# Layer 0 of a graph network on one core: found tiles from two float32r parts of x, four in every batch

## The chip, the core and the metric

The kernel runs on one core of a Trainium2 chip. A core has TensorE (PE, matrix multiply; PEld is its weight load), VectorE (DVE), ScalarE (ACT), GpSimd (POOL, which here issues the indirect DMAs) and SyncE (SP, which issues the plain DMAs). The engines run their own instruction streams and meet at semaphores. The metric is device time in microseconds (us), from one execution to the next; lower is better.

## The reference

12,500 nodes with 32 features and 200,000 edges, sorted by target node. Layer 0 averages the features of the source nodes into each target node; layer 1 is an equivariant message passing whose per-edge weights come from a small network of the edge weight; each layer is followed by a residual and a layer norm.

```
def _L0_gnn_ref(hn, src, dst):
    msgs = hn[src]
    sums = jax.ops.segment_sum(msgs, dst, num_segments=N_NODES)
    deg = jax.ops.segment_sum(jnp.ones((dst.shape[0],), dtype=hn.dtype), dst, num_segments=N_NODES)
    return jnp.where(deg[:, None] > 0, sums / jnp.maximum(deg[:, None], 1.0), 0.0)
...
edge_index = jnp.stack([src, dst])
x = _layernorm(x + _L0_gnn_ref(x, src, dst), axis=-1)
x = _layernorm(x + _L1_gnn_ref(x, edge_weight, edge_attr_3, edge_index, w1, b1, w2, b2), axis=-1)
```

What matters here is `hn[src]`, the row of x for each edge, in float32.

## The kernel before

Each of the 128 partitions owns 1564 consecutive edges, cut into 98 batches of T = 16 edge columns. Batches go in pairs: k = 0 is the even one, k = 1 the odd one. Layer 0 takes 47 pairs in a mixed way, and then two pairs whose rows are all gathered. In a mixed batch some of the 16 tiles (a tile is one column of 128 edges) are gathered from memory by POOL, one indirect DMA of 128 rows each (line 547), and the others are found by TensorE: 3 in an even batch, 4 in an odd one (`FOUND = (3, 4)`), so that POOL gathers 25 a pair.

A found tile is a product with a one-hot matrix. x lies on chip as 128 partitions by 98 nodes. PE first spreads the edges' row codes over the partitions (`spread_codes`, lines 783 and 785, into the bank `rows`). DVE compares them with the block's row numbers and so writes the one-hot `hot_s` (line 1163, into the room `hid`). PE multiplies it with the three bfloat16 parts of x (hi, mid, lo, in the rooms `rest_f`, `inv_len` and `w_sb`), 7 blocks times 3 parts, which makes 21 matmuls of 448 columns into one PSUM bank (`find`, line 800). DVE then multiplies the bank with a second one-hot, `hot_l` (`select`, line 1173), and after the batch's last tile a reduction over it (line 1177) puts the rows into the batch's terms. A carry (line 1241) and a scan along the edges (line 1246) close the batch. PE also counts edges per node with 16 small matmuls a batch (`count`, line 771) out of `hot_p` and `hot_j`, which DVE writes (lines 984 and 986).

Three PSUM banks take found tiles, `found[g % 3]` for the g-th tile of a batch. In an odd batch the fourth tile goes into the first one's bank, so PE waits until that one has been selected (`pe.wait_ge(selected, FOUND_PAIR * i + g + 1)`); in an even batch it waits once, at the first tile, for every earlier selection.

The order of the work is written out by hand. On DVE a batch b is: hot_p, hot_j, hot_l, then hot_s of batch b + 1, then the selections of batch b one after another, the reduction, the carry, the scan. After an odd batch comes a piece of the frames of layer 1 (`frame_piece`, lines 1191 to 1231, one of seven in turn). On PE it is: spread_codes of b + 1, find of b, count of b. POOL issues its gathers in order; those of a batch wait for steps of a find five or so batches earlier (`found_steps`, `AHEAD = 5`), and for their slot, one of seven.

Ahead of the loop x is split: ACT writes hi, DVE writes left = x - hi, mid and lo (`split_x`, lines 1150 to 1155). `w_sb` becomes free for lo only when ACT has copied the last turned block of it (`w_copied`).

Of the kernel before, what the change touches and what calls it, by code (L numbers as in the profile page):

```python
# [25 lines left out]
NPP = 98  # L26
# [8 lines left out]
DEEP = 7  # L35
FOUND = (3, 4)
FETCHED = tuple(T - n for n in FOUND)
FOUND_PAIR = sum(FOUND)
# [49 lines left out]
def build_program(nc, x, src, dst, edge_attr, edge_weight, w1, b1, w2, b2, out):  # L88
    with ExitStack() as ctx:
        def sb(name, shape, dt=F32):  # L90
            return ctx.enter_context(nc.sbuf_tensor(name, shape, dt))
# [7 lines left out]
        def dram(name, shape):  # L99
# [12 lines left out]

        src_all = sb("src_all", [P, COLS + 2 * DEEP * T], I32)
        dst_i = sb("dst_i", [P, COLS], I32)
        dst_f = sb("dst_f", [P, COLS])
        rest_f = sb("rest_f", [P, COLS])
        same = sb("same", [P, COLS])
        unit = sb("unit", [P, COLS, 3])
        inv_len = sb("inv_len", [P, COLS])
        w_sb = sb("w_sb", [P, COLS])  # L120
        x_room = sb("x_room", [P, T * D * MUL])
# [39 lines left out]
        runs_t = [sb(f"runs_t{k}", [P, T, D]) for k in range(2)]  # L161
        frame = [sb(f"frame{k}", [P, T, 3, 3]) for k in range(2)]
        frame_b = [sb(f"frame_b{k}", [P, T, 3, 3]) for k in range(2)]
        hot_p = [sb(f"hot_p{k}", [P, T, P], BF16) for k in range(2)]
        hot_j = [sb(f"hot_j{k}", [P, T, NPP], BF16) for k in range(2)]
        f_along = [sb(f"f_along{k}", [P, T, 2, 2, MUL]) for k in range(2)]
        f_across = [sb(f"f_across{k}", [P, T, 2, 2, MUL]) for k in range(2)]
        hid = [sb(f"hid{k}", [P, T * P]) for k in range(2)]
        halves = [room.rearrange("p (v t o) -> p v t o", t=T, o=D) for room in
# [33 lines left out]
        sq = prod[0][:, :, :, :, :].rearrange("p a b c d -> p (a b c d)")  # L203
        part = sb("part", [P, 3, T, 3, MUL])
        back = sb("back", [P, 3, T, 3, MUL])
        span_room = x1_sb[:, :, :].rearrange("p j f -> p (j f)")
        frame_s = span_room[:, 0:SPAN * 9].rearrange("p (t c a) -> p t c a", c=3, a=3)
        small = span_room[:, SPAN * 9:SPAN * 14].rearrange("p (c t) -> p c t", t=SPAN)
        parts = [room[:, :].bitcast(BF16) for room in (rest_f, inv_len, w_sb)]
        hot_s = [hid[k][:, 0:FOUND[k] * BL * P // 2].bitcast(BF16).rearrange("p (g a e) -> p g a e", g=FOUND[k], a=BL)  # L210
                 for k in range(2)]
        chosen = prod[0][:, :, :, :, :].rearrange("p a b c d -> p (a b c d)")[:, 0:GT * LN * D].rearrange(
# [13 lines left out]
        x_blocks = x_sb[:, :, :].rearrange("p (a l) f -> p a f l", l=LN)  # L226
        hi, mid, lo, left = (room.rearrange("p (a f l) -> p a f l", a=BL, f=D) for room in parts + [span_room])

# [5 lines left out]
        found = [bank[:, 0:LN * D] for bank in (ps_r[:, 1, 0, :], ps_r[:, 1, 2, :], ps_m[:, 1, :])]  # L234
# [29 lines left out]
        parts_ready = sem("parts_ready")  # L264
# [4 lines left out]
        selected = sem("selected")  # L269
# [463 lines left out]
        def _(pe):  # L733
# [4 lines left out]
            with pe.If(unsorted(pe)):  # L738
# [50 lines left out]
            def find(i, k):  # L789

                b = 2 * i + k
                pe.wait_ge(hot_s_ready, b + 1)
                for g in range(FOUND[k]):
                    if k == 1:
                        pe.wait_ge(selected, FOUND_PAIR * i + g + 1)
                    elif g == 0 and (not isinstance(b, int) or b > 0):
                        pe.wait_ge(selected, FOUND_PAIR * i)
                    for a in range(BL):
                        for n, part in enumerate(parts):
                            mm = pe.matmul(found[g % 3], hot_s[k][:, g, a, :], part[:, a * LN * D:(a + 1) * LN * D],  # L800
                                           start=(a == 0 and n == 0), stop=(a == BL - 1 and n == 2))
# [122 lines left out]
        def _(dve):  # L924
            s = Steps(dve, dve_step)
# [220 lines left out]
            def split_x():  # L1146

                dve.wait_ge(loaded_x, 48)
                dve.wait_ge(parts_ready, 1)
                s.mark(dve.tensor_tensor(left, x_blocks, hi, ALU.subtract))  # L1150
                s.settle()
                dve.tensor_copy(mid, left).then_inc(parts_ready, 1)
                dve.wait_ge(parts_ready, 2)
                dve.wait_ge(w_copied, (COLS + P - 1) // P)
                dve.tensor_tensor(lo, left, mid, ALU.subtract).then_inc(parts_ready, 1)

            def make_hot_s(i, k):

                b, n = 2 * i + k, FOUND[k]
                if not isinstance(b, int) or b > 1:  # L1160
                    dve.wait_ge(found_ready, FOUND_PAIR * i - (0 if k else FOUND[1]))
                dve.wait_ge(rows_ready, b + 1)
                dve.tensor_tensor(hot_s[k].rearrange("p g a e -> p a g e"),  # L1163
                                  spread(rows[:, 0:n * P].rearrange("p (g e) -> p g e", g=n), 1, BL),
                                  block_row[:, :].unsqueeze(2).unsqueeze(3).to_broadcast([P, BL, n, P]),
                                  ALU.is_equal).then_inc(hot_s_ready, 1)

            def select(i, k):

                b, n, found_earlier = 2 * i + k, FOUND[k], FOUND_PAIR * i + k * FOUND[0]  # L1170
                for g in range(n):
                    dve.wait_ge(found_ready, found_earlier + g + 1)
                    dve.tensor_tensor(chosen[:, g], found[g % 3].rearrange("p (f l) -> p f l", f=D),  # L1173
                                      spread(hot_l[:, g, :], 1, D), ALU.mult).then_inc(selected, 1)
                dve.wait_ge(selected, found_earlier + n)
                dve.wait_ge(terms1_ready, b + 1)
                s.mark(dve.tensor_reduce(terms0[k][:, :, T - n:T].rearrange("p f g -> p g f"),
                                         chosen[:, 0:n], AX.X, ALU.add))
                s.settle()
# [351 lines left out]
```

## Time and profile before

| | |
|---|---|
| median of 3 runs | 3976.77 us (3973.86 to 3977.89) |
| profiled execution, its own time: first to last instruction | 3977.1 us |
| PE busy (matmuls) | 3526.6 us, 89% |
| DVE busy | 3430.5 us, 86% |
| POOL busy | 2929.9 us, 74% |
| ACT busy | 697.6 us, 18% |

The profile is of one execution. Layer 0 lies in its first 1582 us, and layer 1 in what follows. A busy share is an average over stages with different limits; what bounds a stage is read from which engine waits for which in that stage. PE's matmuls overlap in the record, so their pace is the distance of their starts and not their length. The granted clock is that of TensorE, as a share of its full speed.

### The profile page before, as it was taken

To read this page: it belongs to the slowest core of one execution; us is meant where nothing else is said; L and a number is where in the kernel's file an instruction comes from. 1 tells how busy PE (TensorE), PEld (TensorE's weight loads), DVE (VectorE), ACT (ScalarE), POOL (GpSimd) and SP (SyncE) were. 2 spreads that over 40 slices of the span, in tenths; PEclk is the share of its full clock that TensorE was granted. 3 is DMA by queue.
4 is the path that set the end of the run, shared out by engine and by line. 5 is a ranking of instruction groups with operands and counts; after the bars stand their busy time and mean duration, and the time that the engine had idled before them with its cause. 6 is when DMAs were issued, how large, how long until landed. Compare 5 with 4: busy or idle time off the path is not lost.

```text
span 3977.1 us, 52948 instructions
## 1 busy us (share of the span) xinstructions
PE 3526.6 (89%) x14844; PEld 1886.1 (47%) x14844; DVE 3430.5 (86%) x4447; ACT 697.6 (18%) x1045; POOL 2929.9 (74%) x3010
## 2 busy tenths in 40 slices
PE   5999999999999996349999999999999999999963
PEld 2555555555555543324444444444444444444443
DVE  7888888888888888559999999999999999999965
ACT  1111111111111111002222222222222222222210
POOL 7777777777777776767777777777777777777746
PEclk9999999999999998579999999999999999999975
DMA  3111111111111111122222222222222222222211
GB/s 89 29 42 29 29 43 29 40 30 40 31 40 29 38 31 45 25 42 51 59 53 56 60 57 52 60 55 54 59 54 55 59 58 52 59 57 52 60 32 24
DMA packets 168412, 184.90 MB, mean 46 GB/s; under 512 B 57218, under 2 KB 135685, under 8 KB 161799
## 3 DMA queue, kind: packets, MB, share of 16 engines
q1 hardware_dynamic: 72486, 134.85, 12.1%
q0 software_dynamic: 95840, 49.26, 8.6%
q14 instruction: 76, 0.62, 0.1%
q8 instruction: 10, 0.16, 0.0%
HBM read 121.40 MB, written 62.48 MB: 46 GB/s over the span
## 4 chain that ended last, share of the span: by engine, by line
DVE 20%; PE 17%; issue 12%; DMA 3%; POOL 2%; DVEq 1%; ACT 0%; POOLq 0%
PE ps_r L877 7%; PE ps_m L851 6%; DVE unit L1441 4%; DVE prod L1494 4%; DMA got<-x_d,idx 3%; DVE x_room L1441 3%; DVE part L1464 3%; PE ps_m L868 2%; DVE prod L1486 2%; POOL got L595 1%; DVE back L1428 1%; PE ps_m L835 1%; DVE part L1471 1%; DVE f_across L1475 1%; DVE pick L1367 0%
## 5 line engine op out<-in xcount | busy, mean ns | idle before, releaser
L595 POOL DMA_INDIRECT got<-x_d,idx x1564 | 1559.6, 997 | 534.3 <-issue 354.7
L877 PE MATMUL ps_r<-wc,hid 128*128 128x384 f32 x3128 | 1111.9, 494 | 55.2 <-DVE prod L1494 41.3
L877 PEld LDWEIGHTS ps_r<-wc,hid 128*128 128x128 f32 x3128 | 581.0, 190 | 591.9 <-DVE prod L1494 195.8
L630 ACT COPY runs_t<-runs 128x512 f32<-128x512 f32 x196 | 211.4, 1079 | 2163.1 <-DVE runs L1246 2163.1
L800 PE MATMUL ps_r<-rest_f,hid 128*128 128x448 bf16 x1645 | 585.1, 356 | 0.9 <-DVE prod L1173 0.8
L800 PE MATMUL ps_r<-inv_len,hid 128*128 128x448 bf16 x1645 | 584.4, 355 | 0.0
L800 PE MATMUL ps_r<-w_sb,hid 128*128 128x448 bf16 x1645 | 584.3, 355 | 0.0
L1486 DVE TENSOR_TENSOR prod<-ps_r,f_along 128x768 f32<-128x768 f32 (+1 forms) x586 | 504.1, 860 | 54.2 <-DVE f_across L1475 27.8
L1494 DVE TENSOR_TENSOR prod<-ps_r,f_across 128x768 f32<-128x768 f32 (+1 forms) x586 | 505.8, 863 | 0.0
L547 POOL DMA_INDIRECT got<-in_x_dram,idx_deep x350 | 343.7, 982 | 116.0 <-issue 66.0
L851 PE MATMUL ps_m<-x_room,ident 128*128 128x512 f32 x768 | 379.1, 617 | 54.5 <-DVE x_room L1441 48.4
L851 PE MATMUL ps_m<-unit,ident 128*128 128x512 f32 x784 | 386.9, 618 | 37.0 <-DVE unit L1441 33.8
L547 POOL DMA_INDIRECT f_across<-in_x_dram,idx_deep x357 | 338.5, 948 | 108.8 <-issue 57.3
L547 POOL DMA_INDIRECT f_along<-in_x_dram,idx_deep x353 | 335.2, 950 | 107.6 <-issue 62.8
L1163 DVE TENSOR_TENSOR hid<-ps_r,block_row 128x2688 bf16<-128x2688 f32 x94 | 321.0, 3415 | 0.0
L1173 DVE TENSOR_TENSOR prod<-ps_r,hot_l 128x448 f32<-128x448 f32 x235 | 137.2, 617 | 160.3 <-PE ps_r L800 160.3
L571 POOL DMA_INDIRECT hid<-run_d,pos x196 | 184.9, 943 | 110.2 <-issue 57.0
L1464 DVE TENSOR_TENSOR part<-got,frame 128x384 f32<-128x384 f32 x294 | 179.1, 665 | 93.1 <-DMA got<-x_d,idx 92.4
L1441 DVE TENSOR_TENSOR unit<-prod 128x768 f32<-128x768 f32 (+1 forms) x294 | 254.2, 865 | 0.0
L835 PE MATMUL ps_m<-tail,pick 128*128 128x32 f32 x392 | 88.2, 399 | 186.5 <-DVE pick L1367 186.5
L1441 DVE TENSOR_TENSOR x_room<-prod 128x768 f32<-128x768 f32 (+1 forms) x292 | 253.3, 867 | 0.0
L851 PEld LDWEIGHTS ps_m<-x_room,ident 128*128 128x128 f32 x768 | 146.8, 196 | 220.5 <-issue 174.2
(194 smaller groups left out, 4523.6 us busy)
## 6 DMA issues: line engine op xcount, KB each, us to landing
hid<-weight_t SPq DMA_DIRECT2D x98, 512.0 KB
run_d<-runs_t SPq DMA_DIRECT2D x194, 256.0 KB, 2.1
got<-x_d,idx POOLq DMA_INDIRECT x1564
frame_d<-x_sb SPq DMA_DIRECT2D x7, 1008.0 KB, 5.2
frame<-frame_d SPq DMA_DIRECT2D x98, 72.0 KB
frame_b<-frame_d SPq DMA_DIRECT2D x98, 72.0 KB, 1.9
f_across<-in_x_dram,idx_deep POOLq DMA_INDIRECT x357, 2.4
f_along<-in_x_dram,idx_deep POOLq DMA_INDIRECT x353
```

The lines of the kernel that those rows point to most:

```text
L547: pool.indirect_dma_start(got_deep[k][:, t, :], None, x, bass.IndirectOffsetOnAxis(ap=idx_deep[q][:, k * T + t:k * T + t + 1], axis=0)).th ...
L571: pool.indirect_dma_start(ngot[c % 2][:, c // 2, j - c * NC, :], None, table, bass.IndirectOffsetOnAxis(ap=pos[:, j:j + 1], axis=0)).then_ ...
L595: pool.indirect_dma_start(got[k][:, t, :], None, x1_d, bass.IndirectOffsetOnAxis(ap=idx[k][:, t:t + 1], axis=0)).then_inc(got2_landed[k], 16)
L630: act.copy(runs_t[k][:, :, :], runs[k][:, :, :].rearrange("p f t -> p t f")).then_inc(done, 1)
L800: mm = pe.matmul(found[g % 3], hot_s[k][:, g, a, :], part[:, a * LN * D:(a + 1) * LN * D], start=(a == 0 and n == 0), stop=(a == BL - 1 an ...
L851: mm = pe.matmul(terms2[k].rearrange("p o t -> p t o"), ident[:, :], halves[k][:, v, :, :], start=(v == 0), stop=(v == MUL - 1))
L877: pe.matmul(ps_r[:, g % 2, t, 0:RD], hid[k][:, col:col + P], wc[:, :], start=True, stop=True).then_inc(radial_ready, 1)
L1163: dve.tensor_tensor(hot_s[k].rearrange("p g a e -> p a g e"), spread(rows[:, 0:n * P].rearrange("p (g e) -> p g e", g=n), 1, BL), block_ro ...
L1441: dve.tensor_tensor(halves[k][:, :, FIRST[g]:FIRST[g] + size, :].rearrange("p v t (b u) -> p (t b) v u", u=MUL), prod[q][:, 0:size, :, 0:M ...
L1464: s.mark(dve.tensor_tensor(part[:, c, 0:n], spread(f1[:, :, :, c], 2, 3), spread(frame[k][:, 0:n, c, :], 3, MUL), ALU.mult))
L1486: dve.tensor_tensor(prod[q][:, 0:size, 0:2, :, :], ps_r[:, q, 0:size, 0:256].rearrange("p t (b v u) -> p t b v u", b=2, u=MUL), spread(f_a ...
L1494: dve.tensor_tensor(prod[q][:, 0:size, 2:4, :, :], spread(ps_r[:, q, 0:size, 256:RD].rearrange("p t (v u) -> p t v u", u=MUL), 2, 2), spre ...
```

## The change

Layer 0's found tiles come from two parts of x in the type float32r: ACT writes `x_hi` (x converted to that type) and DVE writes `x_lo` = x - x_hi, in rooms of their own that replace `rest_f`, `inv_len`, `w_sb` and `dst_i` once these are used up. The one-hot `hot_s` becomes float32r too, in a room of its own, with the block index outermost. A found tile is then 7 blocks times 2 parts, 14 matmuls. Both batches of a pair have 4 found tiles (`FOUND = (4, 4)`), and POOL gathers 24 a pair. The three banks are taken in turn over the whole pair (`BANK_OF`: banks 0, 1, 2, 0 in an even batch, 1, 2, 0, 1 in an odd one), and every find of a tile waits for the selection of the tile three before it, which had the same bank. In both batches the fourth tile so waits for the first tile's selection in its own batch. `split_x` is one subtraction instead of three operations, behind the wait for `w_copied`. Several on-chip rooms move (`hid`, `part`, `back`, `frame` now lie where `hot_s` was).

```
-FOUND = (3, 4)
+FOUND = (4, 4)
+BANKS = 3
+BANK_OF = ([g % BANKS for g in range(FOUND[0])], [(g + FOUND[0]) % BANKS for g in range(FOUND[1])])
...
+        x_hi = sb("x_hi", [P, NPP * D], F32R)
+        x_lo = sb("x_lo", [P, NPP * D], F32R)
...
+            hot_s = [in_layer0.enter_context(nc.sbuf_tensor(f"hot_s{k}", [P, BL, FOUND[k], P], F32R)) for k in range(2)]
...
-        parts = [room[:, :].bitcast(BF16) for room in (rest_f, inv_len, w_sb)]
-        hot_s = [hid[k][:, 0:FOUND[k] * BL * P // 2].bitcast(BF16).rearrange("p (g a e) -> p g a e", g=FOUND[k], a=BL)
-                 for k in range(2)]
+        parts = [x_hi[:, :], x_lo[:, :]]
...
                 for g in range(FOUND[k]):
-                    if k == 1:
-                        pe.wait_ge(selected, FOUND_PAIR * i + g + 1)
-                    elif g == 0 and (not isinstance(b, int) or b > 0):
-                        pe.wait_ge(selected, FOUND_PAIR * i)
+                    if k == 1 or g == BANKS:
+                        pe.wait_ge(selected, FOUND_PAIR * i + k * FOUND[0] + g - 2)
+                    elif not isinstance(b, int) or b > 0:
+                        pe.wait_ge(selected, FOUND_PAIR * i - (1, 0, 2)[g])
                     for a in range(BL):
                         for n, part in enumerate(parts):
-                            mm = pe.matmul(found[g % 3], hot_s[k][:, g, a, :], part[:, a * LN * D:(a + 1) * LN * D],
-                                           start=(a == 0 and n == 0), stop=(a == BL - 1 and n == 2))
+                            mm = pe.matmul(found[BANK_OF[k][g]], hot_s[k][:, a, g, :], part[:, a * LN * D:(a + 1) * LN * D],
+                                           start=(a == 0 and n == 0), stop=(a == BL - 1 and n == 1))
...
                 dve.wait_ge(parts_ready, 1)
-                s.mark(dve.tensor_tensor(left, x_blocks, hi, ALU.subtract))
-                s.settle()
-                dve.tensor_copy(mid, left).then_inc(parts_ready, 1)
-                dve.wait_ge(parts_ready, 2)
                 dve.wait_ge(w_copied, (COLS + P - 1) // P)
-                dve.tensor_tensor(lo, left, mid, ALU.subtract).then_inc(parts_ready, 1)
+                dve.tensor_tensor(lo, x_blocks, hi.bitcast(F32), ALU.subtract).then_inc(parts_ready, 1)
```

On DVE, an even batch of the loop, before (`hid` is hot_s of the odd batch that follows, `prod` the selections):

```order
L984 TENSOR_TENSOR hot_p<-ps_r,dst_p 128x2048 [waits hot_counted]
L986 TENSOR_TENSOR hot_j<-ps_r,dst_j 128x1568
L1258 TENSOR_TENSOR hot_l<-ps_r,code_l 128x42
L1163 TENSOR_TENSOR hid<-ps_r,block_row 128x7x4x128 [waits rows_ready,found_ready]
L1173 TENSOR_TENSOR prod<-ps_r,hot_l 128x448 [waits found_ready,scanned,dve_step]
L1173 TENSOR_TENSOR prod<-ps_r,hot_l 128x448 [waits found_ready]
L1173 TENSOR_TENSOR prod<-ps_m,hot_l 128x448 [waits found_ready]
L1177 TENSOR_REDUCE ps_r<-prod 128x3x32 [waits terms1_ready,selected]
L1241 SCALAR_TENSOR_TENSOR ps_r<-runs,same,ps_r 128x32 [waits runs_turned,masks1_ready,dve_step]
L1246 SCALAR_TENSOR_TENSOR runs<-masks,ps_r 128x512 [waits dve_step]
```

The same batch now (`hot_s` is the one-hot):

```order
L991 TENSOR_TENSOR hot_p<-ps_r,dst_p 128x2048 [waits hot_counted]
L993 TENSOR_TENSOR hot_j<-ps_r,dst_j 128x1568
L1261 TENSOR_TENSOR hot_l<-ps_r,code_l 128x56
L1166 TENSOR_TENSOR hot_s<-ps_r,block_row 128x3584 [waits rows_ready,found_ready]
L1176 TENSOR_TENSOR prod<-ps_r,hot_l 128x448 [waits found_ready,scanned,dve_step]
L1176 TENSOR_TENSOR prod<-ps_r,hot_l 128x448 [waits found_ready]
L1176 TENSOR_TENSOR prod<-ps_m,hot_l 128x448 [waits found_ready]
L1176 TENSOR_TENSOR prod<-ps_r,hot_l 128x448 [waits found_ready]
L1180 TENSOR_REDUCE ps_r<-prod 128x4x32 [waits terms1_ready,selected]
L1244 SCALAR_TENSOR_TENSOR ps_r<-runs,same,ps_r 128x32 [waits runs_turned,masks1_ready,dve_step]
L1249 SCALAR_TENSOR_TENSOR runs<-masks,ps_r 128x512 [waits dve_step]
```

The even batch has a fourth selection, whose tile comes from PE behind the first selection; the reduction is 4 tiles wide. The order of the rest is as it was.

On PE, the end of the first even batch before (`ps_m` is the third tile, and after it comes the count):

```order
L800 MATMUL ps_m<-rest_f,hid 128x448
L800 MATMUL ps_m<-inv_len,hid 128x448
L800 MATMUL ps_m<-w_sb,hid 128x448
L771 MATMUL ps_r<-hot_j,hot_p 128x98 [waits hot_ready]
L771 MATMUL ps_r<-hot_j,hot_p 128x98 x15
L783 MATMUL ps_r<-ident_b,code_a 128x128 [waits hot_s_ready]
```

Now, from the end of its third tile on:

```order
L807 MATMUL ps_m<-x_hi,hot_s 128x448
L807 MATMUL ps_m<-x_lo,hot_s 128x448
L807 MATMUL ps_r<-x_hi,hot_s 128x448 [waits selected]
L807 MATMUL ps_r<-x_lo,hot_s 128x448
L807 MATMUL ps_r<-x_hi,hot_s 128x448
```

Behind the third tile stands a fourth one, in the first tile's bank, whose first matmul waits for a selection; the count stands behind its 14 matmuls.

## Rows read from the trace of the kernel before

**Rows 1.** Busy time by stretch, all engines: us (instructions), granted clock, DMA share, GB/s
```profile
600.00:800.00 200.00, 193.69 (x1215) 106.17 (x1214) 169.68 (x152) 28.65 (x39) 151.54 (x160) 0.99 0.15 34
```

**Rows 2.** Waits of VectorE between 92 and 1524 us: total us, times, longest
```profile
DVE prod L1173 <- PE ps_r L800: 150.6, 45, 3.3
DVE prod L1173 <- PE ps_m L800: 21.1, 40, 2.5
```

**Rows 3.** VectorE, one pair of batches: start us, us, what ran [idle before]
```profile
817.83 2.29 DVE L984 TENSOR_TENSOR hot_p<-ps_r,dst_p 128x2048 bf16<-128x2048 f32 x1 [0.24 <-DVE x_sb L1206]
...
821.84 3.88 DVE L1163 TENSOR_TENSOR hid<-ps_r,block_row 128x3584 bf16<-128x3584 f32 x1
825.64 1.15 DVE L1173 TENSOR_TENSOR prod<-ps_r,hot_l 128x448 f32<-128x448 f32 x2
...
827.35 1.56 DVE L1177 TENSOR_REDUCE ps_r<-prod 128x96 f32<-128x1344 f32 x1
...
834.50 2.95 DVE L1163 TENSOR_TENSOR hid<-ps_r,block_row 128x2688 bf16<-128x2688 f32 x1
...
842.77 0.62 DVE L1173 TENSOR_TENSOR prod<-ps_r,hot_l 128x448 f32<-128x448 f32 x1 [3.35 <-PE ps_r L800]
843.42 2.03 DVE L1177 TENSOR_REDUCE ps_m<-prod 128x128 f32<-128x1792 f32 x1
...
847.03 1.53 DVE L1209 RECIPROCAL x_sb<-x_sb 128x224 f32<-128x224 f32 x1
```

**Rows 4.** Timeline of VectorE, the second pair's first instruction
```profile
92.07 2.28 DVE L984 TENSOR_TENSOR hot_p<-ps_r,dst_p 128x2048 bf16<-128x2048 f32 x1
```

**Rows 5.** Timeline of VectorE, the 47th pair's first instruction
```profile
1523.70 2.29 DVE L984 TENSOR_TENSOR hot_p<-ps_r,dst_p 128x2048 bf16<-128x2048 f32 x1
```

**Rows 6.** Timeline of all engines at the end of a four-tile batch
```profile
811.25 0.35 PE L800 MATMUL ps_r<-inv_len,hid 128*128 128x448 bf16 x1
...
811.44 0.35 PE L800 MATMUL ps_r<-w_sb,hid 128*128 128x448 bf16 x1
...
811.63 0.89 PE L771 MATMUL ps_r<-hot_j,hot_p 128*128 128x98 bf16 x16
811.83 0.63 DVE L1173 TENSOR_TENSOR prod<-ps_r,hot_l 128x448 f32<-128x448 f32 x1 [3.35 <-PE ps_r L800]
...
812.84 0.35 PE L800 MATMUL ps_r<-rest_f,hid 128*128 128x448 bf16 x1
```

**Rows 7.** Timeline of TensorE around a gap of the loop
```profile
503.85 0.90 PE L771 MATMUL ps_r<-hot_j,hot_p 128*128 128x98 bf16 x16 [0.30 <-DVE hot_j L986]
507.84 0.23 PE L783 MATMUL ps_r<-ident_b,code_a 128*128 128x128 bf16 x1 [3.09 <-DVE hid L1163]
...
509.74 0.58 PE L800 MATMUL ps_r<-inv_len,hid 128*128 128x448 bf16 x1
510.11 0.58 PE L800 MATMUL ps_r<-w_sb,hid 128*128 128x448 bf16 x1
...
512.59 0.35 PE L800 MATMUL ps_r<-rest_f,hid 128*128 128x448 bf16 x1
```

**Rows 8.** Waits of TensorE between 92 and 1524 us
```profile
PE ps_r L783 <- DVE hid L1163: 35.8, 37, 3.1
```

**Rows 9.** Timeline of TensorE in the second layer, float32 matmuls
```profile
1999.83 3.39 PE L877 MATMUL ps_r<-wc,hid 128*128 128x384 f32 x10
```

**Rows 10.** The costliest groups of the page: count, busy us, mean ns, idle before
```profile
L877 PEld LDWEIGHTS ps_r<-wc,hid 128*128 128x128 f32 x3128 | 581.0, 190 | 591.9 <-DVE prod L1494 195.8
```

**Rows 11.** Timeline of VectorE before the first pair
```profile
38.80 5.53 DVE L1150 TENSOR_TENSOR x_sb<-x_room,rest_f 128x3136 f32<-128x3136 f32 x1 [6.67 <-ACT rest_f L619]
...
46.63 3.43 DVE L1155 TENSOR_TENSOR w_sb<-x_sb,inv_len 128x3136 bf16<-128x3136 f32 x1 [0.47 <-ACT wt_out L623]
50.09 2.96 DVE L1163 TENSOR_TENSOR hid<-ps_r,block_row 128x2688 bf16<-128x2688 f32 x1
52.96 2.28 DVE L984 TENSOR_TENSOR hot_p<-ps_r,dst_p 128x2048 bf16<-128x2048 f32 x1
```

More of the change, by code:

```diff
@@ L8 @@
 BF16 = mybir.dt.bfloat16
+F32R = mybir.dt.float32r
 I32 = mybir.dt.int32
@@ L57 @@
 N_REST = N - LAST * NPP
+SPARE_ROOM = max(1, BL * sum(FOUND) * P - 2 * T * P - 2 * 3 * T * 3 * MUL - 4 * T * 9)
 C_SS = 0.25
@@ L113, in build_program @@
         src_all = sb("src_all", [P, COLS + 2 * DEEP * T], I32)
-        dst_i = sb("dst_i", [P, COLS], I32)
+        with ExitStack() as before_layers:
+            rest_f, inv_len, w_sb = (before_layers.enter_context(nc.sbuf_tensor(name, [P, COLS], F32))
+                                     for name in ("rest_f", "inv_len", "w_sb"))
+            dst_i = before_layers.enter_context(nc.sbuf_tensor("dst_i", [P, COLS], I32))
+        x_hi = sb("x_hi", [P, NPP * D], F32R)
+        x_lo = sb("x_lo", [P, NPP * D], F32R)
         dst_f = sb("dst_f", [P, COLS])
-        rest_f = sb("rest_f", [P, COLS])
         same = sb("same", [P, COLS])
         unit = sb("unit", [P, COLS, 3])
-        inv_len = sb("inv_len", [P, COLS])
-        w_sb = sb("w_sb", [P, COLS])
         x_room = sb("x_room", [P, T * D * MUL])
@@ L153, in build_program @@
         b1_col = sb("b1_col", [H, 1])
+        with ExitStack() as in_layer0:
+            hot_s = [in_layer0.enter_context(nc.sbuf_tensor(f"hot_s{k}", [P, BL, FOUND[k], P], F32R)) for k in range(2)]
+        hid = [sb(f"hid{k}", [P, T * P]) for k in range(2)]
+        part = sb("part", [P, 3, T, 3, MUL])
+        back = sb("back", [P, 3, T, 3, MUL])
+        frame = [sb(f"frame{k}", [P, T, 3, 3]) for k in range(2)]
+        frame_b = [sb(f"frame_b{k}", [P, T, 3, 3]) for k in range(2)]
+        spare_room = sb("spare_room", [P, SPARE_ROOM])
         idx = [sb(f"idx{k}", [P, T], I32) for k in range(2)]
@@ L161, in build_program @@
         runs_t = [sb(f"runs_t{k}", [P, T, D]) for k in range(2)]
-        frame = [sb(f"frame{k}", [P, T, 3, 3]) for k in range(2)]
-        frame_b = [sb(f"frame_b{k}", [P, T, 3, 3]) for k in range(2)]
         hot_p = [sb(f"hot_p{k}", [P, T, P], BF16) for k in range(2)]
@@ L167, in build_program @@
         f_across = [sb(f"f_across{k}", [P, T, 2, 2, MUL]) for k in range(2)]
-        hid = [sb(f"hid{k}", [P, T * P]) for k in range(2)]
         halves = [room.rearrange("p (v t o) -> p v t o", t=T, o=D) for room in
@@ L203, in build_program @@
         sq = prod[0][:, :, :, :, :].rearrange("p a b c d -> p (a b c d)")
-        part = sb("part", [P, 3, T, 3, MUL])
-        back = sb("back", [P, 3, T, 3, MUL])
         span_room = x1_sb[:, :, :].rearrange("p j f -> p (j f)")
@@ L226, in build_program @@
         x_blocks = x_sb[:, :, :].rearrange("p (a l) f -> p a f l", l=LN)
-        hi, mid, lo, left = (room.rearrange("p (a f l) -> p a f l", a=BL, f=D) for room in parts + [span_room])
+        hi, lo = (room.rearrange("p (a f l) -> p a f l", a=BL, f=D) for room in parts)
         iota = ps_r[:, 1, 1, 0:P]
@@ L815, in _ @@
             spread_codes(0, 0)
-            pe.wait_ge(parts_ready, 3)
+            pe.wait_ge(parts_ready, 2)
             layer0(0, True, False)
@@ L1162, in make_hot_s @@
                 dve.wait_ge(rows_ready, b + 1)
-                dve.tensor_tensor(hot_s[k].rearrange("p g a e -> p a g e"),
+                dve.tensor_tensor(hot_s[k][:, :, :, :],
                                   spread(rows[:, 0:n * P].rearrange("p (g e) -> p g e", g=n), 1, BL),
@@ L1172, in select @@
                     dve.wait_ge(found_ready, found_earlier + g + 1)
-                    dve.tensor_tensor(chosen[:, g], found[g % 3].rearrange("p (f l) -> p f l", f=D),
+                    dve.tensor_tensor(chosen[:, g], found[BANK_OF[k][g]].rearrange("p (f l) -> p f l", f=D),
                                       spread(hot_l[:, g, :], 1, D), ALU.mult).then_inc(selected, 1)
@@ L1284, in _ @@
             split_x()
-            dve.wait_ge(parts_ready, 3)
             dve.wait_ge(codes_ready, 4)
```

## The prediction

> **What bounds the kernel now.** The change touches layer 0's loop of 47 pairs and what leads up to it, so I read that stretch alone. Three engines run there almost without a pause, and the question is which one has room. Busy time by stretch first: in 200 us PE is busy 194 us, DVE 170, and POOL issues 160 gathers [rows 1]. That is 1.25 us a gather, so 25 a pair take POOL 31.2 us, and it has no pause either. The pair itself is read off DVE: from the first instruction of the second pair to that of the 47th there are 45 pairs, (1523.70 - 92.07) / 45 = 31.81 us each [rows 4, 5].
>
> The waits say who holds whom. DVE waits for found tiles for 150.6 + 21.1 = 171.7 us, 3.82 us a pair [rows 2], nearly all in one place: ahead of the odd batch's fourth tile, 3.35 us a time [rows 3]. PE at that time is not waiting; it works through 21 matmuls at a pace of 0.19 us, 4.0 us a tile [rows 6]. PE waits for DVE 35.8 us over the whole stretch, 37 times [rows 8]. So before, PE sets the pair's time, with DVE close behind: without waits DVE needs 31.81 - 3.82 = 27.99 us a pair.
>
> **The change, part by part.**
>
> *Matmuls.* 147 a pair become 8 x 14 = 112, 35 x 0.19 = 6.6 us less, if a float32r matmul goes at the pace of the bfloat16 one. No row shows float32r. The nearest rows below are the same 448 columns in bfloat16, 0.19 us [rows 6]; above, the float32 ones, ten instructions in 3.39 us with the last one 0.49 long, 0.32 us for 384 columns, so 0.376 for 448 [rows 9], and there are 3128 of them [rows 10] for the 1564 matmuls of the program (98 batches of 16 tiles less 4 in the last), so one float32 product may cost twice that, 0.75. I take 0.19, the row of the same shape, and keep the others as a rival. The Trainium skill, FP8 and Floating Point Precision, TensorE Precision Notes, says that true float32 takes four passes, while the reduced form reads four bytes and cuts them to its own width; one pass would give the sum below at 0.19, four the far rival, and the rows here show only that float32 itself is dear. The weight load is 0.19 us in float32 [rows 10], just the pace, so it hides behind the matmul before; if it did not, a matmul would be 0.38, the same rival. The Trainium skill, TensorE: Matmul & The Clock Gate, LDWEIGHTS (loading the stationary operand), counts one column per 1.2 GHz cycle, an estimate of 107 ns for 128, and in Weight-path perf modes — Fast Weight Load (FWL) and DoubleRow denies float32 the fast load; by it an unhidden load makes 0.30 us a matmul, and the time 4215, inside my range.
>
> *DVE.* The even batch gets a fourth tile: hot_s 3.88 instead of 2.95, one selection more at 0.62, a reduction of 2.03 instead of 1.56 [rows 3]. That is 0.93 + 0.62 + 0.47 = 2.02 us a pair, and DVE without waits comes to 30.01. I price the float32r hot_s at the bfloat16 one's 3.88: it reads the same float32 bank, element by element. Its bounds are the other side's rival below and the slowest float32 row, 5.53 us for 3136 elements read with a stride [rows 11], 1.76 ns an element, which would be 6.3 us; hot_s is not strided, so I leave that end out of the sum.
>
> *The new wait.* In both batches the fourth tile waits for the first one's selection, and that stands on DVE behind hot_p, hot_j, hot_l and hot_s. Follow one batch from the moment the fourth tile is there (select starts 0.39 us after its last matmul, 811.83 [rows 6]). DVE: selection to the end of the scan 847.03 - 842.77 = 4.26; hot_p to the next batch's first selection 825.64 - 817.83 = 7.81 [rows 3]; that selection 0.62; a hand-over, for which I take 0.2 from the 0.24 idle that DVE's own hand-overs show [rows 3]. Sum 12.89. PE meanwhile: count and codes 812.84 - 811.63 = 1.21 [rows 6], three tiles 3 x 2.66 = 7.98, together 9.19, begun 0.20 earlier than DVE. So PE stands idle 12.89 + 0.20 - 9.19 = 3.9 us in each batch, longer by the frame piece after an odd one. Then tile four takes 13 x 0.19 + 0.39 = 2.86 to DVE, which has two selections to do meanwhile, 1.71 - 0.62 = 1.09 [rows 3]; it waits 0.2 + 2.86 - 1.09 = 1.97 us, twice a pair. Queued behind this wait are the fourth selection, reduction, carry and scan, and the whole next batch. Before, the odd batch had this wait too, but PE came to it late: its three tiles before took 12 us.
>
> With the clock up a pair takes 30.01 + 3.94 = 33.95 us. The old wait of 3.82 is gone, and 3.94 are back.
>
> *The clock.* Seven gaps of PE in this stretch were 2.4 to 3.1 us long, two of them side by side. Behind each of these six places matmuls went at 0.37 us instead of 0.19, which is 1.2 GHz instead of 2.4; at the one shown they do from its end at 507.84 to about 512.4 [rows 7]. Over the six the low level held for 3.0 to 5.6 us behind the gap, 3.9 in the mean. Behind the 22 gaps between 0.4 and 1.2 us it was never seen. The new gap of 3.9 us and more is longer than all of them, and tile four, on DVE's chain, is what follows it: 3.9 us at 0.37 are 10.5 matmuls, the other 3.5 take 0.67, so 4.57 instead of 2.66, 1.9 us a batch. With 3.0 us it is 1.45, with the whole tile slow 2.5. A pair is 33.95 + 3.8 = 37.75, between 36.9 and 39.0.
>
> *POOL.* 24 gathers a pair, 30.0 us. It is no longer near the bound, and its gathers wait for steps of finds as DVE's chain lets these come. The gain of 1.25 a pair isn't seen.
>
> *Before and behind the loop.* x_lo is one subtraction, 5.53 us [rows 11], that now stands behind ACT's last copy, at 46.6 (before, only the last of three operations did). It ends at 52.1 instead of 46.63 + 3.43 = 50.1, and the first hot_s has 4 tiles, 0.93 more: 3 us later. The conversion on ACT and the longer code split lie in DVE's 6.67 us wait for ACT [rows 11]. First pair: slow PE clock before and after, no change. The last pair, without a hot_s in its odd batch, about 1 us more. Layer 1 keeps its instructions.
>
> Sum: 45 x (37.75 - 31.81) = 267, and 3 + 1: 271 us. The profiled execution's span is 3977.1, with nothing around it, 0.3 from the runs' median of 3976.8, so 4248 us. The clock's bounds, 36.9 and 39.0, give 4210 and 4305.
>
> **The rivals.**
>
> *The clock stays up, or falls in a part of the gaps.* For: six places are few, and none of them follows another within a batch, as the new gaps do. Against: it fell at all six. All up: 45 x 2.14 + 4 = 100, 4077 us; falls only behind a frame piece, once a pair: 35.85, 4163 us.
>
> *PE stays the bound at a float32r pace of 0.376.* For: float32's rows, and the load's 0.19. Then 112 x 0.376 + 2 x 1.21 = 44.5 a pair, the gaps are gone, 45 x 12.7 + 4: 4552 us. At 0.75 it would be 86.4 and some 6430. A pace in between, 0.25 to 0.30, lands near my forecast by another way: tile four grows by 0.8 to 1.5 us, while the gap shrinks and the clock stays.
>
> *Faster: hot_s is written straight through.* Before, its blocks and tiles were written crosswise, now in one run. If that halves it, 1.94 us a batch come off the chain, and a pair is 33.95 - 3.88 = 30.07, just over POOL's 30.0; the gap is 2.0 us, under the shortest after which the clock fell. 45 x (30.07 - 31.81) + 4: 3902 us. It decides from 1.07 us saved per hot_s on. Against: lo, written straight through, took 3.43 us for 3136 elements [rows 11], 1.09 ns each, and hot_s 3.88 for 3584, 1.08 each; no crosswise loss is seen.
>
> **How the numbers follow.** The forecast 0.62; the clock up in all or part 0.17; PE the bound 0.12; hot_s faster 0.05; something that cancels to within 0.2%, which is about what a measurement of this kernel tells from no change, 0.04. The range reaches from a little under the rival with the clock up to a little over the slow bound, 4060 to 4330; it leaves out the last three, 0.21 less what of a middle pace falls within. The forecast alone is 4210 to 4305. Faster 0.05, same 0.04, slower 0.91.
>
> **What would show it.** Right: hot_p of every second batch 37 to 39 us apart; DVE waiting for tile four in both batches, about 3.9 us each; PE's first matmul of tile four behind a wait for a selection of 3.9 us or more; matmuls of that tile 0.37 apart, of the next three 0.19; about 127 gathers in 200 us; x_lo ending near 52. Wrong: a PE without gaps (the pace of float32r), gaps with matmuls at 0.19 behind them (the clock), a hot_s far from 3.88, or POOL again without pauses.

## The result, and the profile after

The kernel with the change takes 4255.85 us in the median (4251.74 to 4261.65, four runs), the one before on the same chip 3975.66 (3973.86 to 3977.89): 1.0708 times as long [1.0695, 1.0721], 280 us slower. The profiled execution has a span of 4250.0 us, 272.9 more than that of before; it is the fastest of the four (4251.74). The forecast was 4248.

First the costliest groups of the page that the change made: line, engine, operation, count, then busy us, mean ns of one, idle time before and what ended it.

```profile
L807 PE MATMUL ps_r<-x_hi,hot_s 128*128 128x448 f32 x1974 | 846.4, 429 | 388.4 <-DVE prod L1176 388.4
L807 PEld LDWEIGHTS ps_r<-x_hi,hot_s 128*128 128x128 f32 x1974 | 444.7, 225 | 464.4 <-DVE prod L1176 422.7
L1176 DVE TENSOR_TENSOR prod<-ps_r,hot_l 128x448 f32<-128x448 f32 x282 | 170.3, 618 | 371.5 <-PE ps_r L807 371.4
L1166 DVE TENSOR_TENSOR hot_s<-ps_r,block_row 128x3584 fp32r<-128x3584 f32 x94 | 364.8, 3881 | 0.0
```

Read the last columns of lines one and three together. PE waits 388 us for a selection on DVE, and DVE waits 371 us for found tiles from PE: each waits for the other in turn, which neither busy share tells. The same 200 us as in [rows 1], busy time by engine (PE, PEld, DVE, ACT, POOL, with instructions), granted clock, DMA share and GB/s:

```profile
600.00:800.00 200.00, 156.11 (x836) 137.81 (x835) 154.29 (x132) 26.58 (x35) 121.55 (x129) 0.86 0.12 25
```

PE fell from 193.7 to 156.1 us, DVE from 169.7 to 154.3, POOL from 160 gathers to 129, and the granted clock from 0.99 to 0.86. Nothing is a full engine any more. The waits of DVE and of PE in the loop's stretch (95 to 1800 us: total us, times, longest), which answer to [rows 2, 8]:

```profile
DVE prod L1176 <- PE ps_r L807: 360.1, 90, 4.6
```

```profile
PE ps_r L807 <- DVE prod L1176: 380.8, 90, 10.9
```

Ninety waits are two a pair over 45 pairs: 4.00 us on DVE, 4.23 on PE. POOL, which before (92 to 1524 us) waited 0.3 us at the longest ahead of a gather into `f_across`, now waits for up to 8.6 us until PE's finds have gone on:

```profile
POOL f_across L547 <- PE ps_r L800: 35.4, 116, 0.3
```

```profile
POOL f_across L554 <- PE ps_r L807: 128.7, 123, 8.6
```

One pair on DVE, where [rows 3] showed one of before (start us, us, what ran, idle before):

```profile
999.18 2.29 DVE L991 TENSOR_TENSOR hot_p<-ps_r,dst_p 128x2048 bf16<-128x2048 f32 x1 [0.24 <-DVE x_sb L1214]
...
1003.21 3.88 DVE L1166 TENSOR_TENSOR hot_s<-ps_r,block_row 128x3584 fp32r<-128x3584 f32 x1
1007.00 1.14 DVE L1176 TENSOR_TENSOR prod<-ps_r,hot_l 128x448 f32<-128x448 f32 x2
1008.07 0.61 DVE L1176 TENSOR_TENSOR prod<-ps_m,hot_l 128x448 f32<-128x448 f32 x1
1012.83 0.62 DVE L1176 TENSOR_TENSOR prod<-ps_r,hot_l 128x448 f32<-128x448 f32 x1 [4.15 <-PE ps_r L807]
...
1030.28 0.62 DVE L1176 TENSOR_TENSOR prod<-ps_r,hot_l 128x448 f32<-128x448 f32 x1 [3.71 <-PE ps_r L807]
...
1036.59 2.29 DVE L991 TENSOR_TENSOR hot_p<-ps_r,dst_p 128x2048 bf16<-128x2048 f32 x1 [0.24 <-DVE x_sb L1221]
```

And PE in the same pair, around the even batch's fourth tile:

```profile
1001.72 0.36 PE L807 MATMUL ps_m<-x_hi,hot_s 128*128 128x448 f32 x1
1001.92 0.36 PE L807 MATMUL ps_m<-x_lo,hot_s 128*128 128x448 f32 x1
1007.67 0.74 PE L807 MATMUL ps_r<-x_hi,hot_s 128*128 128x448 f32 x1 [5.39 <-DVE prod L1176]
1008.21 0.57 PE L807 MATMUL ps_r<-x_lo,hot_s 128*128 128x448 f32 x1
1008.58 0.57 PE L807 MATMUL ps_r<-x_hi,hot_s 128*128 128x448 f32 x1
...
1012.22 0.37 PE L807 MATMUL ps_r<-x_hi,hot_s 128*128 128x448 f32 x1
1012.42 0.37 PE L807 MATMUL ps_r<-x_lo,hot_s 128*128 128x448 f32 x1
```

Tile three goes at 0.20 us a matmul. PE then stands 5.39 us, until DVE, at 1007.00, comes from hot_s to the first selection; tile four begins at 0.37 a matmul (1.2 GHz) and is back at 0.20 (2.4 GHz) from 1012.22 on. DVE, which needs it, waits 4.15. The granted clock of that stretch is 0.51:

```profile
1007.60:1012.20 4.60, 4.53 (x12) 4.05 (x13) 1.08 (x3) 0.00 (x0) 1.30 (x2) 0.51 0.02 4
```

Before the loop, to be set against [rows 11]:

```profile
45.51 5.57 DVE L1158 TENSOR_TENSOR x_lo<-x_room,x_hi 128x3136 fp32r<-128x3136 f32 x1 [13.41 <-ACT wt_out L630]
51.00 3.88 DVE L1166 TENSOR_TENSOR hot_s<-ps_r,block_row 128x3584 fp32r<-128x3584 f32 x1
54.80 2.28 DVE L991 TENSOR_TENSOR hot_p<-ps_r,dst_p 128x2048 bf16<-128x2048 f32 x1
```

The second pair's hot_p starts at 91.73 and the 47th's at 1800.42: 37.97 us a pair, against 31.81 [rows 4, 5]. 45 x 6.16 = 277 us, and the ends give back 4.

### The profile page after: what moved, and what is told of

The parts are those of the page before. It is cut to its first block, busy times and chain, and to the rows that moved or that the text cites. A ratio compares the mean times of both kernels' runs of the same rounds, so it can differ in the third digit from the quotient of the medians.

```text
span 4250.0 us, 49966 instructions
## 1 busy us (share of the span) xinstructions
PE 3457.0 (81%) x13293; PEld 2313.7 (54%) x13293; DVE 3517.2 (83%) x4492; ACT 701.1 (16%) x1045; POOL 2881.8 (68%) x2963
## 4 chain that ended last, share of the span: by engine, by line
DVE 19%; PE 16%; issue 11%; DMA 3%; POOL 2%; DVEq 1%; ACT 0%; POOLq 0%
PE ps_r L884 7%; PE ps_m L858 6%; DVE prod L1496 4%; DVE unit L1443 4%; DMA got<-x_d,idx 3%; DVE x_room L1443 3%; DVE part L1466 2%; DVE prod L1488 2%; PE ps_m L875 2%; POOL got L602 1%; DVE back L1430 1%; PE ps_m L842 1%; DVE part L1473 1%; DVE f_across L1477 1%; DVE ps_m L1244 0%
## 5 line engine op out<-in xcount | busy, mean ns | idle before, releaser
L807 PE MATMUL ps_r<-x_hi,hot_s 128*128 128x448 f32 x1974 | 846.4, 429 | 388.4 <-DVE prod L1176 388.4
L807 PE MATMUL ps_r<-x_lo,hot_s 128*128 128x448 f32 x1974 | 822.1, 416 | 0.0
L807 PEld LDWEIGHTS ps_r<-x_hi,hot_s 128*128 128x128 f32 x1974 | 444.7, 225 | 464.4 <-DVE prod L1176 422.7
L1176 DVE TENSOR_TENSOR prod<-ps_r,hot_l 128x448 f32<-128x448 f32 x282 | 170.3, 618 | 371.5 <-PE ps_r L807 371.4
L554 POOL DMA_INDIRECT f_across<-in_x_dram,idx_deep x344 | 329.0, 956 | 198.7 <-PE ps_r L807 130.8
L807 PEld LDWEIGHTS ps_r<-x_lo,hot_s 128*128 128x128 f32 x1974 | 441.3, 224 | 40.0
L554 POOL DMA_INDIRECT got<-in_x_dram,idx_deep x336 | 326.8, 972 | 197.2 <-PE ps_r L807 119.5
L554 POOL DMA_INDIRECT f_along<-in_x_dram,idx_deep x340 | 322.0, 947 | 189.1 <-PE ps_r L807 122.8
L1166 DVE TENSOR_TENSOR hot_s<-ps_r,block_row 128x3584 fp32r<-128x3584 f32 x94 | 364.8, 3881 | 0.0
L858 PEld LDWEIGHTS ps_m<-unit,ident 128*128 128x128 f32 x784 | 149.2, 195 | 207.9 <-issue 164.1
```

What stands on the lines that cost most here:

```text
L554: pool.indirect_dma_start(got_deep[k][:, t, :], None, x, bass.IndirectOffsetOnAxis(ap=idx_deep[q][:, k * T + t:k * T + t + 1], axis=0)).th ...
L807: mm = pe.matmul(found[BANK_OF[k][g]], hot_s[k][:, a, g, :], part[:, a * LN * D:(a + 1) * LN * D], start=(a == 0 and n == 0), stop=(a == B ...
L858: mm = pe.matmul(terms2[k].rearrange("p o t -> p t o"), ident[:, :], halves[k][:, v, :, :], start=(v == 0), stop=(v == MUL - 1))
L1166: dve.tensor_tensor(hot_s[k][:, :, :, :], spread(rows[:, 0:n * P].rearrange("p (g e) -> p g e", g=n), 1, BL), block_row[:, :].unsqueeze(2) ...
L1176: dve.tensor_tensor(chosen[:, g], found[BANK_OF[k][g]].rearrange("p (f l) -> p f l", f=D), spread(hot_l[:, g, :], 1, D), ALU.mult).then_in ...
```

## The experiments

"Pair" below is the distance of two pairs' hot_p, as above; each ratio is to the kernel before on the same chip.

**fill: keep TensorE busy in the gap.** Extra bfloat16 matmuls stand ahead of tile four's wait; the wait itself stays. They write into unused columns of the bank in which the counts are summed, and this kernel gives up a right result for it (whether it is the counts that change is not shown). Only its time is used.

```
+                        if g == BANKS:
+                            for _ in range((65, 30)[k]):
+                                pe.matmul(ps_r[:, 0, 0, 256:256 + P], ident_b[:, :], ident_b[:, :], start=True, stop=True, skip_group_check=True)
                     if k == 1 or g == BANKS:
                         pe.wait_ge(selected, FOUND_PAIR * i + k * FOUND[0] + g - 2)
```

> The changed kernel with PE kept busy in its gap: ahead of the fourth tile's wait PE runs 65 (even batch) or 30 (odd batch) extra 128-column bfloat16 matmuls into unused columns, 3.6 and 1.7 us at full clock. If the low clock behind the gap costs tile four 1.9 us a batch, a pair goes from 37.8 to about 34 us, the time to 4080 us (4070 to 4150, if some gaps stay long), and tile four's matmuls stand 0.2 us apart. If the clock were not on the path (the wait alone makes the loss), the time stays at 4256 or rises.

4103.65 us, 1.0319 [1.0302, 1.0336]; a pair 34.49. Its 200 us, its waits of DVE (95 to 1650 us) and the start of a fourth tile on PE:

```profile
600.00:800.00 200.00, 181.95 (x1472) 165.15 (x1471) 164.46 (x146) 26.89 (x36) 130.34 (x137) 0.98 0.12 31
```

```profile
DVE prod L1179 <- PE ps_r L810: 204.0, 90, 4.6
```

```profile
1008.25 1.85 PE L804 MATMUL ps_r<-ident_b 128*128 128x128 bf16 x30
1011.30 0.47 PE L810 MATMUL ps_r<-x_hi,hot_s 128*128 128x448 f32 x1 [1.19 <-DVE prod L1179]
1011.61 0.37 PE L810 MATMUL ps_r<-x_lo,hot_s 128*128 128x448 f32 x1
1011.81 0.36 PE L810 MATMUL ps_r<-x_hi,hot_s 128*128 128x448 f32 x1
```

The clock is 0.98 and tile four goes at 0.20. A wait of DVE falls from 4.00 to 204.0 / 90 = 2.27 us in the mean. This mean is mixed: in 83 of the 90 batches tile four went at 0.20 throughout and DVE waited 2.11 us, and in the other 7 the clock still fell and it waited 4.06. So 152 of the 280 us are the clock, a little less than the whole of it (an estimate from the waits: 90 x (4.00 - 2.11) = 170), and the wait at full clock is enough to keep the kernel 3% slower than before.

**early: the first selection ahead of hot_s.** Only DVE's order changes: the selection that frees tile four's bank no longer stands behind the 3.88 us of hot_s.

```
-                    if not (last and k == 1):
-                        make_hot_s(i + k, 1 - k)
...
-                    select(i, k)
+                    select(i, k, (0,))
+                    if not (last and k == 1):
+                        make_hot_s(i + k, 1 - k)
+                    select(i, k, range(1, n))
```

> The changed kernel with one thing moved on DVE: the first tile's selection stands ahead of the next hot_s instead of behind it, 3.9 us earlier. If the loss is the fourth tile's wait for that selection, tile four is found while DVE writes hot_s, the wait goes, PE's gap shrinks below 2 us and the clock stays up: a pair takes DVE's own 30.0 us, 3900 us in all (3885 to 3935), under the kernel before. If PE's float32r matmuls or DVE's added work made the loss, the time stays above 4150.

3912.86 us, 0.9835 [0.9818, 0.9851]: 343 us under the change as it stood, and 1.6% under the kernel before. A pair takes 30.27. Busy time by stretch, the waits of DVE for tiles (95 to 1500 us), and two gaps of PE:

```profile
600.00:800.00 200.00, 179.58 (x1040) 159.06 (x1039) 189.17 (x165) 31.53 (x42) 151.31 (x160) 0.94 0.14 36
```

```profile
DVE prod L1176 <- PE ps_r L807: 3.9, 4, 2.1
```

```profile
1000.21 0.47 PE L807 MATMUL ps_r<-x_hi,hot_s 128*128 128x448 f32 x1 [2.41 <-DVE prod L1176]
1000.52 0.36 PE L807 MATMUL ps_r<-x_lo,hot_s 128*128 128x448 f32 x1
1000.72 0.36 PE L807 MATMUL ps_r<-x_hi,hot_s 128*128 128x448 f32 x1
...
1030.25 0.74 PE L807 MATMUL ps_r<-x_hi,hot_s 128*128 128x448 f32 x1 [2.38 <-DVE prod L1176]
1030.79 0.57 PE L807 MATMUL ps_r<-x_lo,hot_s 128*128 128x448 f32 x1
1031.16 0.57 PE L807 MATMUL ps_r<-x_hi,hot_s 128*128 128x448 f32 x1
```

DVE's 360 us of waiting are 3.9. The gap below 2 us and the clock that stays up, both expected, did not come: PE still waits 58 times for a selection, 2.26 us in the mean, and behind 27 of these gaps matmuls of the tile went at 0.37. But tile four now has hot_s's 3.88 us to arrive in, and even at the low clock that nearly covers it. POOL is back at 160 gathers in 200 us, which makes 24 x 1.25 = 30.0 a pair, and DVE is at 95%.

**banks4: a fourth bank instead.** Tile four gets a bank of its own, the one in which the constant `iota` lay; iota moves to SBUF, and DVE's order stays.

```
-BANKS = 3
+BANKS = 4
...
+        iota_room = sb("iota_room", [P, P])
...
-        iota = ps_r[:, 1, 1, 0:P]
+        iota = iota_room[:, :]
...
-        found = [bank[:, 0:LN * D] for bank in (ps_r[:, 1, 0, :], ps_r[:, 1, 2, :], ps_m[:, 1, :])]
+        found = [bank[:, 0:LN * D] for bank in (ps_r[:, 1, 0, :], ps_r[:, 1, 2, :], ps_m[:, 1, :], ps_r[:, 1, 1, :])]
...
-                    if k == 1 or g == BANKS:
-                        pe.wait_ge(selected, FOUND_PAIR * i + k * FOUND[0] + g - 2)
-                    elif not isinstance(b, int) or b > 0:
-                        pe.wait_ge(selected, FOUND_PAIR * i - (1, 0, 2)[g])
+                    if not isinstance(b, int) or b > 0:
+                        pe.wait_ge(selected, FOUND_PAIR * i + k * FOUND[0] + g - 3)
```

> The changed kernel with a fourth PSUM bank for found tiles, made free by keeping the row of numbers that hot_p is compared with (iota) in SBUF; DVE's order stays. A tile then waits for the selection four tiles back, which is always of an earlier batch. If the loss is the third bank's reuse, DVE no longer waits for tile four and a pair takes 30 to 30.5 us: 3900 us (3885 to 3935), although PE still idles and its clock still falls, since that is off the path then. If the clock itself were the loss, the time stays above 4100. If an SBUF operand makes hot_p or hot_j slower or faster than 2.28 and 1.78 us, 94 times the difference comes on top.

4098.66 us, 1.0306 [1.0289, 1.0323], a pair 33.38: a miss. The wait for found tiles is gone, as expected; what DVE waits for now (95 to 1600 us) are gathered rows, which ACT passes on:

```profile
DVE ps_m L1179 <- ACT ps_m L643: 117.6, 37, 3.5
DVE ps_r L1179 <- ACT ps_r L643: 33.8, 32, 2.1
```

POOL issues 142 gathers in 200 us here and yet is busy for 157 us of them. I had priced the move of iota for hot_p and hot_j alone, and not for POOL. By itself this run does not show what a fourth bank is worth; that it would stand near early without the price of iota is an estimate from the next run (4099 less 190).

**early_iota: the move of iota alone.** early, with its three banks, and only iota in SBUF.

```
+        iota_room = sb("iota_room", [P, P])
...
-        iota = ps_r[:, 1, 1, 0:P]
+        iota = iota_room[:, :]
```

> The early kernel (3913 us, three banks) with iota in SBUF as in the kernel with four banks, and nothing else changed. If the SBUF operand of hot_p is what slowed POOL's gathers there (mean 1.11 us instead of 0.95 in the profile), the time is that of four banks, 4085 to 4115, with DVE waiting for gathered rows and not for found tiles. If four banks themselves did it, it stays at 3913.

4103.36 us, 1.0316 [1.0299, 1.0333], a pair 33.47: 190 us more than early for the place of one constant. Timeline of DVE and POOL in early_iota:

```profile
1015.12 1.29 POOL L555 DMA_INDIRECT f_along<-in_x_dram,idx_deep  x1 [0.30 <-PE ps_r L808]
...
1016.43 2.28 DVE L992 TENSOR_TENSOR hot_p<-iota_room,dst_p 128x2048 bf16<-128x2048 f32 x1
...
1016.72 2.82 POOL L555 DMA_INDIRECT f_along<-in_x_dram,idx_deep  x1 [0.30 <-PE ps_m L808]
1018.63 1.79 DVE L994 TENSOR_TENSOR hot_j<-iota_room,dst_j 128x1568 bf16<-128x1568 f32 x1
1019.84 1.40 POOL L555 DMA_INDIRECT f_along<-in_x_dram,idx_deep  x1 [0.30 <-issue]
...
1021.54 0.94 POOL L555 DMA_INDIRECT f_along<-in_x_dram,idx_deep  x1 [0.30 <-issue]
```

The gather begun beside hot_p takes 2.82 instead of 0.94 us and ends at 1019.54, 0.83 behind the end of hot_p (1018.71). The next one ends at 1021.24, 0.82 behind the end of hot_j (1020.42). hot_p keeps its own 2.28, so it is the gather that stands still. All 188 gathers begun beside hot_p or hot_j between 95 and 1660 us took 1.39 us or more; in early, where iota lies in PSUM and hot_p has one SBUF input, all 302 of them between 95 and 1500 us took 0.94 to 0.96. The Trainium skill, SBUF — State Buffer, Who interferes with whom, has the rule: a VectorE instruction with two inputs in SBUF reads its second one through the interface that it shares with GpSimd, and contends there with a GpSimd instruction that reads SBUF; the shared ports are an exclusive lock. The two ends above agree with it.

**bf16_44: the schedule without float32r.** The three bfloat16 parts of before, with four found tiles in each batch and the banks in turn. The edit is to the kernel before:

```
-FOUND = (3, 4)
+FOUND = (4, 4)
+BANKS = 3
+BANK_OF = ([0, 1, 2, 0], [1, 2, 0, 1])
...
-                    if k == 1:
-                        pe.wait_ge(selected, FOUND_PAIR * i + g + 1)
-                    elif g == 0 and (not isinstance(b, int) or b > 0):
-                        pe.wait_ge(selected, FOUND_PAIR * i)
+                    if k == 1 or g == BANKS:
+                        pe.wait_ge(selected, FOUND_PAIR * i + k * FOUND[0] + g - 2)
+                    elif not isinstance(b, int) or b > 0:
+                        pe.wait_ge(selected, FOUND_PAIR * i - (1, 0, 2)[g])
...
```

> The kernel before (three bfloat16 parts, 21 matmuls a tile) with four found tiles in every batch and the banks in turn, so float32r undone alone. If the wait for the first selection sets the pair, it takes 30.0 + 2 x 3.3 = 36.5 us, since tile four takes 4.2 us to DVE and the gap ahead of it is short, so that the clock stays up: 4195 us (4170 to 4260). If float32r is what costs, this kernel stays near 3980 or below.

4209.75 us, 1.0581 [1.0563, 1.06], a pair 36.79. With 21 matmuls a tile instead of 14 it is 46 us faster than the change. Its 200 us, and its waits of DVE from 95 to 1760 us:

```profile
600.00:800.00 200.00, 189.81 (x1208) 103.63 (x1205) 160.68 (x141) 26.93 (x37) 126.34 (x133) 1.00 0.10 26
```

```profile
DVE prod L1175 <- PE ps_r L802: 310.4, 90, 6.0
```

The wait is there in both batches without any float32r, 3.45 us a time. PE's gaps are short, since three tiles take it 12 us (it waits for a selection 45 times in that stretch, 92.9 us in all), and the clock stays up. So here the kernel in which PE has more to do loses less by this order.

**bf16_early: bf16_44 with early's order.**

> Four found tiles in every batch out of three bfloat16 parts (float32r undone), with the first selection ahead of hot_s. The wait is then covered, and PE bounds the pair: 168 x 0.19 + 2 x 1.21 = 34.3 us, without gaps, clock up: 4090 us (4075 to 4110). If float32r brought nothing once the wait is gone, this kernel would be at 3913 like its float32r twin.

4093.65 us, 1.03 [1.0283, 1.0317], a pair 34.35:

```profile
600.00:800.00 200.00, 199.03 (x1266) 109.45 (x1265) 168.17 (x147) 26.62 (x36) 132.55 (x140) 1.00 0.13 33
```

Its waits of PE for a selection, from 95 to 1640 us:

```profile
PE ps_r L802 <- DVE prod L1175: 6.9, 5, 3.7
```

PE is busy 199 of 200 us at full clock, and 168 matmuls at 0.19 with two counts of 1.21 [rows 6] are 34.3 a pair: PE alone sets it. So of bf16_44's 234 us 116 were the wait, and 118 are left with PE as the bound: it has 21 more matmuls a pair than before, 4.0 us, of which the pair of 31.81 had room for 1.5. Between bf16_early and early lie 181 us: what the 14 matmuls are worth once the wait is covered.

**three_four: the change with three found tiles in the even batch.** POOL gathers 25 a pair again, and only the odd batch has the wait.

```
-FOUND = (4, 4)
+FOUND = (3, 4)
...
-BANK_OF = ([g % BANKS for g in range(FOUND[0])], [(g + FOUND[0]) % BANKS for g in range(FOUND[1])])
+BANK_OF = ([0, 1, 2], [0, 1, 2, 0])
...
-                        pe.wait_ge(selected, FOUND_PAIR * i - (1, 0, 2)[g])
+                        pe.wait_ge(selected, FOUND_PAIR * i - (0, 2, 1)[g])
```

> The changed kernel with the old split of 3 and 4 found tiles (25 gathered a pair), the three banks in turn over 7 tiles: float32r alone. The even batch has no reuse of a bank within itself, so only the odd one keeps the wait: DVE's 28.0 us and one wait of 2 to 4 us make 30.1 to 32.0 a pair, POOL's 25 gathers 31.2. That is 3950 to 3985 us, like the kernel before. If float32r itself cost or gained time on the path, it would stand well outside 3940 to 3995.

3971.05 us, 0.9987 [0.9978, 0.9997], a pair 31.13. float32r matmuls with the split of before change the time by 0.1%.

**early34: three_four with early's order.** It was to show whether that one wait still costs anything.

> The same 3 and 4 split in float32r with the first selection ahead of hot_s: no wait is left on DVE (28.0 us a pair), PE needs 98 x 0.2 + 2.4 = 22 us, so POOL's 31.2 us bound the pair: 3950 us (3940 to 3960). Against the early kernel with 4 and 4 (3913) it says what the 25th gather costs: 45 x 1.25 = 56 us if POOL alone bounds, less if DVE's 30.0 us does there.

3971.05 us again, 0.9988 [0.9978, 0.9997]: 11 above the upper end of what was expected. Its 200 us, and then the last gather of layer 0 on POOL's timeline, in the kernel before, in early34 and in early:

```profile
600.00:800.00 200.00, 159.65 (x902) 142.89 (x903) 172.00 (x154) 32.02 (x42) 151.55 (x160) 0.86 0.15 36
```

```profile
1571.31 0.94 POOL L547 DMA_INDIRECT pick<-in_x_dram,idx_deep  x1 [0.30 <-issue]
```

```profile
1570.16 0.94 POOL L554 DMA_INDIRECT pick<-in_x_dram,idx_deep  x1 [0.30 <-issue]
```

```profile
1513.04 0.94 POOL L554 DMA_INDIRECT pick<-in_x_dram,idx_deep  x1 [0.30 <-issue]
```

PE and DVE both have time left, and still a pair takes 31.08: POOL's 160 gathers in 200 us set it, and the kernel before ends its stream of them 1 us later. DVE's waits for found tiles (95 to 1500 us) fell from 110.6 us in three_four to 38.4, and the time is the same, so that one wait costs nothing here. The expected 3950 is 0.6 us off each of 45 pairs of the kernel before. But in that kernel POOL had no pause over 0.32 us from its first gather at 13.54 us to its last at 1571.31, and the same holds in three_four, early34 and early: 1235 gathers, or 1188 in early, at 1.26 us each. It is this whole stream that ends layer 0. early34 and early differ by 58.2 us, and one gather a pair is 47 x 1.25 = 58.7.

## Why the prediction was right, step by step

**The bound before.** That PE sets the time was wrong for layer 0 as a whole. PE had little room, and the distance of DVE's pairs was its pace, but POOL had none at all: with PE relieved (early34) the pair goes only from 31.81 to 31.08, and the whole kernel by 5 us. The prediction read POOL's 31.2 in [rows 1] and then went on with PE alone. For the sum this did no harm, since the change left both with room, and DVE's chain set the pair (POOL stands for up to 8.6 us there). It did matter for the value of the idea: the 6.6 us of PE's that it saves were worth nothing by themselves, and the one gather less was worth 59.

**The pace of float32r.** Taken 0.19, measured 0.20, in one instruction. The rivals at 0.376 and more are out, and so is an unhidden weight load: it takes 225 ns in the mean here and doesn't show in the pace.

**DVE.** Taken 30.01 without waits; 37.97 less 2 x 4.00 is 29.97. hot_s takes 3.881 against 3.88, so the rival with a faster hot_s is out. Its other half, that a chain with less on it brings the kernel to POOL's bound, is what early shows by moving hot_s instead (3902 worked out, 3913 measured).

**The new wait.** 1.97 us a batch at full clock, measured 2.11 in the 83 batches of fill whose clock stayed up. Two errors stand against each other in it. The tile takes 3.11 us from its first matmul to DVE (1011.30 to 1014.41) where I had 2.86: 0.13 is the pace, and 0.11 the first matmul, which is followed after 0.31 us. And the hand-over from DVE to PE, taken as 0.2, is 0.06 there (the selection that frees the bank ends at 1010.63 + 0.61 = 1011.24, and tile four begins at 1011.30). What is left is 0.14 x 90 = 13 us, the largest error in the pair. The rival with the clock up, 4077, is 27 under fill's 4104; these 13 and the 7 batches with a low clock, 7 x 1.95 = 14, make that up.

**The clock.** 1.9 us a batch, measured 4.00 - 2.11 = 1.89. Tile four had matmuls at 0.37 in all 90 batches of the stretch; the forecast had six places to go by. PE's gaps are 4.23 us in the mean where I had 3.9 in each batch and more behind a frame piece: 5.51 ahead of the fourth tiles of the even batches, behind such a piece, and only 2.95 in the odd ones. The low pace lasts about 4.6 and 3.7 us in the pair shown, 3.9 taken. fill, which holds the clock up in most batches, wins 152 us (171 were worked out, 45 x 3.8).

**The ends.** Three us were added for the start; it is 1.84, since ACT's last copy came earlier and x_lo, 5.57 long, could begin at 45.51 instead of 46.6. The first pair I left unchanged; it is 36.93 instead of 39.11. Behind the 47th pair's start 4 us come back, where I had one more. I did not follow these two up.

**POOL.** 129 gathers in 200 us, about 127 forecast, each batch's held up by finds that come later.

The terms of the loop, wait, clock and DVE, came out to within 0.14 us a batch; the agreement of the whole sum to 2 us is luck. The pair is 0.22 us longer than forecast (+10 us on 45), the ends are 8 shorter, and so 271 us were forecast and 272.9 measured between the two profiled executions. The measured median, 4255.85, is 8 us above the forecast.

## What to carry to other kernels

When a buffer is used again within one round, look at what stands ahead of the operation that frees it on the freeing engine: here one 0.62 us selection behind 3.88 us of work that nobody waited for yet cost 343 us, and changing the places of the two made the loss a gain. A shorter stream on an engine that two others keep up with brings nothing until those get shorter too, so list every engine without pauses before pricing a relief. A constant moved to another memory is not free: count what the instructions that read it now share with other engines.

## What was not expected of the hardware

- float32r went through TensorE in one instruction at 0.20 us for 448 columns, the same to 0.01 us as bfloat16 [rows 6], while the float32 matmul of layer 1 takes two (3128 instructions [rows 10] for 1564 products). The weight load is 197 ns in early and 99 in bf16_44, and neither shows in the pace.
- Gaps of one length need not end alike: in early one of 2.41 us was followed by matmuls at 0.20 us, and one of 2.38, thirty us later, by matmuls at 0.37. One of 2.99 us (ahead of 970.15) kept the clock, and one of 1.96 (ahead of 1152.16) lost it, so the prediction's 2.0 us, under the shortest gap after which it had seen the clock fall, was not safe.
- With iota in SBUF indirect DMAs of the loop took up to 3.04 us to issue, against 0.94, and POOL's mean went from 0.95 to 1.12 us.
